# Four-layer GNN on one core: the first layer's edge stage in another order on ACT and DVE, and half of the prelude's one-hots of the high index part on POOL

## What is computed

```python
h = relu(layernorm(x))
x = x + L0(h, src, dst)      # degree-normalised convolution, l2 norm, tanh
h = relu(layernorm(x))
x = x + L1(h, ...)           # two relational attention layers
h = relu(layernorm(x)); x = x + L2(h, ...)
h = relu(layernorm(x)); x = x + L3(h, ...)

# L0
src_, dst_ = src + self loops, dst + self loops
deg  = segment_sum(ones, src_)          # a count of edges by source node
norm = rsqrt(deg)
agg  = segment_sum((h @ W)[src_] * norm[src_], dst_) * norm[:, None]
out  = tanh(agg / max(l2(agg), 1e-12))
```

## Time and profile before

| what | value |
|---|---|
| median of 3 runs | 4407.27 us (4401.42 to 4411.29) |
| the profiled execution | 4407.76 us, span 4406.1 us |
| mean granted TensorE clock | 0.829 |
| busy in the span | PE 68%, PEld 38%, DVE 78%, ACT 49%, POOL 47% |
| `prelude`, about 45 to 245 us | histogram loop 51 to 222 us |
| `layer0_edges`, about 597 to 1380 us | first scan 606.9 us, last `pq` 1372.0 us |

### The profile page before, as it was taken

One profiled execution on the slowest core, in us unless ns is written; L12 is line 12 of the kernel. 1 busy time (PEld: TensorE's weight loads), 2 busy tenths in 40 slices (PEclk: granted clock), 3 DMA queues, 4 the chain that ended last, 5 costly groups with the idle time before them and its releaser, 6 DMA issues. The chain is left out here.

```text
span 4406.1 us, 66823 instructions
## 1 busy us (share of the span) xinstructions
PE 2981.6 (68%) x12342; PEld 1689.0 (38%) x12342; DVE 3436.7 (78%) x10172; ACT 2152.9 (49%) x5600; POOL 2066.3 (47%) x1915
## 2 busy tenths in 40 slices
PE   5966644333344999567999322888887999707886
PEld 1255533222232444223444111544444666503443
DVE  6989968888886888675555686799995666698997
ACT  0058866666663222153212265677774666404554
POOL 0045567777774654005554000555555555204776
PEclk9967767777666999778999655899998999858999
DMA  2079966666663222174322297344444656503332
GB/s 51 2 223 309 310 212 225 212 210 213 212 225 101 68 63 59 24 213 118 64 62 57 79 246 203 101 131 123 128 126 149 201 192 198 163 0 114 114 113 87
DMA packets 621057, 628.07 MB, mean 143 GB/s; under 512 B 167332, under 2 KB 494590, under 8 KB 614468
## 3 DMA queue, kind: packets, MB, share of 16 engines
q1 hardware_dynamic: 572900, 523.78, 39.6%
q0 software_dynamic: 48000, 102.76, 9.5%
HBM read 333.97 MB, written 296.91 MB: 143 GB/s over the span
## 5 line engine op out<-in xcount | busy, mean ns | idle before, releaser
L1417 PE MATMUL r_pM<-r_masked,wr 128*128 128x512 f32 x1600 | 750.3, 622 | 55.3 <-DVE r_masked L1368 55.2
L1368 DVE SCALAR_TENSOR_TENSOR r_masked<-r_typ,r_hT 128x512 f32<-128x512 f32 x800 | 493.5, 687 | 239.9 <-ACT r_hT L1395 189.0
L1417 PEld LDWEIGHTS r_pM<-r_masked,wr 128*128 128x128 f32 x1600 | 308.8, 199 | 427.3 <-issue 298.5
L1259 PE MATMUL e_pY<-ident,e_agg 128*128 128x128 f32 x400 | 134.1, 439 | 406.8 <-DVE e_agg L1134 381.6
L741 POOL DMA_INDIRECT q_rows<-nr,row_x x200 | 258.0, 1290 | 194.8 <-PE q_pT L590 134.6
L2445 POOL DMA_INDIRECT out<-o_base,o_at_o x200 | 266.7, 1333 | 133.8 <-issue 66.3
L1259 PEld LDWEIGHTS e_pY<-ident,e_agg 128*128 128x128 f32 x400 | 107.0, 327 | 418.6 <-issue 234.5
L741 POOL DMA_INDIRECT r_xs<-tab,r_at_s x200 | 216.4, 1082 | 87.9 <-issue 46.3
L741 POOL DMA_INDIRECT r_xs<-h_tab,r_at_s x200 | 215.7, 1079 | 87.8 <-issue 47.0
L590 PE MATMUL g_pT<-ident,g_hT 128*128 128x128 f32 x400 | 95.2, 381 | 230.0 <-ACT g_hT L1799 177.1
L741 POOL DMA_INDIRECT i_hs<-hr,i_at_s x200 | 191.1, 956 | 88.0 <-issue 47.5
(11 more groups left out here) (416 smaller groups left out, 8943.0 us busy)
## 6 DMA issues: line engine op xcount, KB each, us to landing
xz<-na_xz SPq DMA_DIRECT2D x49, 1040.0 KB, 5.8
r_typ<-vec_s SPq DMA_DIRECT2D x100, 256.0 KB, 3.4
g_al<-alpha_s SPq DMA_DIRECT2D x100, 256.0 KB, 4.1
na_xz<-in_x SPq DMA_DIRECT2D x49, 512.0 KB, 7.0
tab<-na_x SPq DMA_DIRECT2D x49, 512.0 KB
e_xin<-tab SPq DMA_DIRECT2D x49, 512.0 KB
hr<-e_hh SPq DMA_DIRECT2D x49, 512.0 KB, 3.7
zh_s<-e_zh SPq DMA_DIRECT2D x49, 512.0 KB
```

What stands on the lines that cost most here:

```text
L1259: pe.matmul(pY[s][:, cols], agg[s][:, cols], g.ident[:, :], start=True, stop=False)
L1368: v.scalar_tensor_tensor(masked[:, r, :], typ[d.slot(4)][:, :], float(r), hT[d.slot(2)][:, :], ALU.is_equal, ALU.mult).then_inc(ev.mk, 1)
L1417: pe.matmul(pM[s][:, :], g.wr[:, layer * R_ + r, :], masked[:, r, :], start=(r == 0), stop=(r == R_ - 1)).then_inc(ev.mm, 1)
```

## The change

In `prelude` the loops on DVE and PE are written out for all 200 tiles. DVE no longer makes `hi1` of side 1. POOL makes it, one instruction per tile, once DVE has signalled the parts (`s_parts`) and, from tile 8 on, PE has done with the slot. PE waits for POOL's `s_hi` before side 1's product.

In `layer0_edges` the order of a turn changes on two engines. On DVE the pair's `n` moves behind `x1`, `sx` and `mx`. On ACT the chain `et` moves ahead, right behind `hh`; then come `hTx`, `rz`, `rh`, `by_dst`, the squares, and `pq` last. The waits of each step move with it.

```diff
@@ prelude
+        @block.gpsimd
+        def _(pool):
+            wait_alone(g, pool, s_parts, 1)
+            for t in range(T):
+                if t >= PER:
+                    wait_alone(g, pool, s_mm, 2 * (t - PER) + 2)
+                pool.tensor_scalar(hi1[:, t % PER, 1, :], g.iota_lo[:, 0:P], part[:, 0, 1, t:t + 1], None, ALU.is_equal).then_inc(s_hi, 1)
...
-            v.sem_inc(s_cmp, 2 * PER)
-            with v.Fori(0, T // PER) as i:
-                for k in range(PER):
-                    for side in range(2):
-                        v.wait_ge(s_mm, i * 2 * PER + 2 * k + side + 1)
-                        v.tensor_scalar(hi1[:, k, side, :], ...)
-                        v.tensor_scalar(lo1[:, k, side, :], ...).then_inc(s_cmp, 1)
+            v.sem_inc(s_parts, 1)
+            for t in range(T):
+                k = t % PER
+                for side in range(2):
+                    if t >= PER:
+                        v.wait_ge(s_mm, 2 * (t - PER) + side + 1)
+                    if side == 0:
+                        v.tensor_scalar(hi1[:, k, side, :], ...)
+                    v.tensor_scalar(lo1[:, k, side, :], ...).then_inc(s_cmp, 1)
...
+            for t in range(T):
+                k = t % PER
+                for side in range(2):
+                    if side == 1:
+                        pe.wait_ge(s_hi, t + 1)
+                    pe.wait_ge(s_cmp, 2 * t + side + 1)
+                    pe.matmul(ph[:, side, :], hi1[:, k, side, :], lo1[:, k, side, :], start=False, stop=False).then_inc(s_mm, 1)
@@ layer0_edges, DVE
-                if n2:
-                    ... normalise(v, hh[s][:, of(m), :], mvh[:, of(m), :], rh[:, of(m)], n_[s][:, of(m), :], nd.nn)
                 if e2:
                     ... x1, stats(v, c, g, x1[s], sx, mx, ed.sx)
+                if n2:
+                    ... normalise(...), as above
                 if n1:
                     ... nm
@@ layer0_edges, ACT (order within a turn)
-  rx, ri, by_src, hh, hTx, pq, rh, et, by_dst + squares, rz
+  rx, ri, by_src, hh, et, hTx, rz, rh, by_dst + squares, pq
```

More of the change, by code:

```diff
@@ L396, in prelude @@
         g.sem("nn_" + n) for n in ("zh", "cmp", "mm", "all", "vec", "deg", "norm", "sum", "pre", "row", "out", "turned"))
+    s_parts, s_hi = g.sem("nn_parts"), g.sem("nn_hi")
     PER = 8
@@ L494, in _ @@
             c.step(v.tensor_copy(part[:, :, :, :], part_i[:, :, :, :]))
-            v.sem_inc(s_cmp, 2 * PER)
-            with v.Fori(0, T // PER) as i:
-                for k in range(PER):
-                    for side in range(2):
-                        v.wait_ge(s_mm, i * 2 * PER + 2 * k + side + 1)
-                        v.tensor_scalar(hi1[:, k, side, :], g.iota_lo[:, 0:P], part[:, 0, side, bass.ds(i * PER + k, 1)], None, ALU.is_equal)
-                        v.tensor_scalar(lo1[:, k, side, :], g.iota_lo[:, :], part[:, 1, side, bass.ds(i * PER + k, 1)], None,
-                                        ALU.is_equal).then_inc(s_cmp, 1)
+            v.sem_inc(s_parts, 1)
[5 more added lines that the diff above has]
+                    if side == 0:
+                        v.tensor_scalar(hi1[:, k, side, :], g.iota_lo[:, 0:P], part[:, 0, side, t:t + 1], None, ALU.is_equal)
+                    v.tensor_scalar(lo1[:, k, side, :], g.iota_lo[:, :], part[:, 1, side, t:t + 1], None, ALU.is_equal).then_inc(s_cmp, 1)
             v.wait_ge(s_all, 2)
@@ L1171, in turn @@
                     stats(v, c, g, x1[s], sx, mx, ed.sx)
+                if n2:
+                    s = n2.slot(2)
+                    v.wait_ge(nd.rh, n2.one())
+                    if n2.k >= 2:
+                        v.wait_ge(w_n[s], 16 * n2.uses(2))
+                    for m in MEMBERS:
+                        normalise(v, hh[s][:, of(m), :], mvh[:, of(m), :], rh[:, of(m)], n_[s][:, of(m), :], nd.nn)
                 if n1:
@@ L1209, in turn @@
                         last.then_inc(nd.hh, 1)
[L1210 to L1222, removed]
                 if e2:
@@ L1230, in turn @@
                     a.activation(et[:, :, :], et[:, :, :], ACT.Exp, scale=-1.0, bias=g.log2_col[:, :]).then_inc(ed.r2, 1)
+                if e3:
+                    a.wait_ge(ed.tx, e3.now())
+                    a.wait_ge(ed.pq, e3.back(1))
+                    a.activation(hTx[:, :], pX[:, :], ACT.Relu).then_inc(ed.hx, 1)
+                if n1:
+                    a.wait_ge(nd.sz, n1.one())
+                    a.wait_ge(nd.hh, n1.back(1))
+                    rstd(a, g, c, mvz, rz, nd.rz)
+                if n2:
+                    a.wait_ge(nd.sh, n2.one())
+                    a.wait_ge(nd.nn, n2.back(1))
+                    rstd(a, g, c, mvh, rh, nd.rh)
                 if e1:
@@ L1239, in turn @@
                     last.then_inc(ed.ss, 1)
[L1240 to L1243, removed]
+                if e3:
+                    a.wait_ge(ed.pq, e3.now())
+                    if e3.k >= 2:
+                        a.wait_ge(w_q[e3.slot(2)], 16 * e3.uses(2))
+                    a.activation(pq[e3.slot(2)][:, :], pX[0:R_, :], ACT.Copy).then_inc(ed.pe, 1)
             braid.sweep(a, turn, c)
```

## The result

| | before | after | ratio, 95% interval |
|---|---|---|---|
| median | 4404.35 us (4 runs) | 4332.84 us (4 runs, 4325.94 to 4334.71) | 0.9833, 0.9815 to 0.985 |
| profiled execution, its span | 4407.76, 4406.1 us | 4331.46, 4329.7 us | |
| histogram loop, first low one-hot to last product | 51.2 to 221.6 us | 50.6 to 209.9 us | |
| woven stage, first scan to last `pq` | 765.1 us | 698.3 us | |
| last `pq` to the end | 3034.0 us | 3036.3 us | |

The span is 76.4 us shorter: 66.8 us in the woven stage, 11 us in the histogram loop, and nothing elsewhere beyond 2.3 us.

A forecast was written before the change was run, and what follows sets the result against it. DVE was taken as the bound in the histogram loop and woven stage, with 0.92 us a turn lost to ACT's order. 4407.8 - 69 (woven stage: -47 - 7 - 15) + 18 (prelude) = 4357 us, range 4305 to 4410.

The forecast's parts named there:

- DVE waits, -47: Woven stage: DVE's waits of `n` for `rh` and `x1` for `et` go in ordinary turns, minus 47 us, from 0.
- The end, -7: Last turns of the woven stage: with `et` first, DVE waits less for `rh` and `et`, minus 7 us, from 0 to 10.
- a new wait of about 0.8: Woven stage, turn before the last: the 3.3 us wait shrinks to about 0.8, giving 2.5 us.
- The loop, -15: DVE's loop branch in the woven stage: `n`'s eight instructions ahead of it cover part of the 3.9 us stall, minus 15 us.
- head start of 1.7 us: Woven stage: DVE's sequencer meets the branch before DVE is done, worth 1.7 us a pass, at most 2.2.
- Prelude, +18: Histogram loop: DVE loses one one-hot but pays 0.25 us for POOL's, 0.94 us a tile, plus 18 us over 200 tiles.
- rival B: Prelude costs more than the woven stage gives: at 1.3 us a tile 90 us longer, 4429 us; chance 0.12.
- ratio 0.84: Prelude: share of POOL's instruction that DVE can't overlap, 1.07/1.27, applied to an assumed 0.30 us.
- every case of two memory-reading instructions shown has them exclude each other: Prelude: reason for taking plus 18 us, between bounds of -33 us without exclusion and +88 us.
- Rival A: Prelude: DVE's and POOL's streams don't exclude each other, -33 in place of +18, 4306 us; chance 0.15.
- Rival C: Woven stage: POOL is the new bound, no turn under 13.3 us, 4388 us; chance 0.13.
- Rival D: Woven stage: the loop's stall goes altogether as written-out prelude code shifts the body, 20 us more, 4337 us; chance 0.10.

The follow-up runs named there:

- experiment 2: Kernel before with only DVE's new order in the woven stage: 4491.28 us; with only ACT's new order: 4378.15 us.
- Experiment 6: Changed kernel, POOL making three of four high one-hots, ACT's `rz` and `rh` ahead of `hTx` in turns without a new block: 4415.04 us, ratio 0.9967, other chip.
- experiment 4: With both on POOL: changed kernel, POOL making both high one-hots of every tile, DVE only the low ones: 4492.77 us on another chip.

## Why the prediction was right, point by point

**4357 us was forecast, 4333 measured**, inside 4305 to 4410, the woven stage as reckoned and the prelude with the wrong sign. The prelude was missed by 29 us, more than the whole; the range held that by its width:

| term | forecast | measured |
|---|---|---|
| waits of `n` and `x1`, the ordinary turns and the end | -47 - 7 = -54 | 35.2 + 21.8 - 8.1 - 2.6 = -46.3 |
| wait behind the branch | -15 | 34.8 - 23.2 = -11.6 |
| not in the sum: `nm` -7.0, `ssw` +4.8, DVE busy -7.6 | 0 | -9.8 |
| small waits | 0 | +0.9 |
| woven stage | -69 | -66.8 |
| prelude | +18 | -11 (0.806 against 0.863 per tile) |

- *DVE waits, -47.* Right, in mechanism and size: an ordinary turn lost 1.0 us (forecast 0.92), and experiment 2 shows that each order takes its own part and that DVE's half is a loss of 84 us without ACT's.
- *The end, -7.* Half of it. With the ordinary turns nearly clean, what is left of both waits (8.1 and 2.6) lies at the stage's ends: from the last scan to the last `pq` it went from 30.5 to 26.8 us, 3.7. The step that failed is "a new wait of about 0.8" for `n`: it was 3.86, since ACT comes to `rh` only behind `hTx`, and that waited 4.97 us for PE. Experiment 6 adds that the whole term could not be had by order: the stage's end follows the last gather.
- *The loop, -15.* The mechanism was right: the stall of about 4 us starts when the branch goes out and DVE's queued work covers part of it. So was the head start of 1.7 us: DVE's queued work ended 0.14 us behind the branch's start before, and 1.84 us behind it now. The term that failed is the stall itself, which the sum left as it was: from the branch's start to the sequencer's next record it is 4.30 us in the mean of nine now and was 3.89, so that 11.6/9 = 1.3 us a pass is left of the 1.7. It is 4.30 us with ACT's order alone too; why it grew stays open.
- *Missed rows.* One wait of 7.6 us of `nm` for `rz` was in the waits of before and in no step of the sum; moving `rz` ahead took it. And `z` beside `zh` lost less.
- *Prelude, +18.* Wrong, by two errors that pull apart. POOL's instruction is 0.60 us, not 0.30, which by the forecast's own formula would have been 0.69 + 0.50 = 1.19 us a tile and a loss of 68 us, the point at which rival B begins to win. But the ratio 0.84 is also wrong for this pair: it was taken from float32 sums of 128x512 and moved to fp16 comparisons. Measured it is 0.11/0.60. The step that failed is "every case of two memory-reading instructions shown has them exclude each other": the rows showed two pairs, neither of this form. In one of the two turns of rows 6 `z` kept its 1.28 us and it was POOL's `zh` that took 3.35, so even there DVE did not always pay. What came in its place is a shared pace of 0.79 us a tile, with 0.11 us lost to DVE.
- *Rival A* (no exclusion, -33) was the nearer one for the prelude: a third of its gain came. *Rival B* is the case of experiment 4 with both on POOL: there the pace is 1.26 us and the loop 82 us longer than before, near B's 90, with POOL as the bound and not the round trip that B described. *Rival C*: in the turns without a stall POOL has no gap either, with 8 gathers at 0.95 + 0.30 and 2.78 + 0.15 for `zh`, 12.9 us; the 13.3 of the forecast held a stretched `zh`. So POOL and DVE end together at 12.9 to 13.0, and the next gain in this stage has to shorten both. *Rival D*, the shifted code, did not happen in the changed kernel and did in two of the experiments on the first chip, whose stages are 24 and 29 us shorter; its time, 4337, is close to the result by chance.

## What to carry to other kernels

When a change reorders two engines, run each half alone: here one half of a good change makes the stage 84 us longer. DVE's loop body of 326 records paid about 4 us of its sequencer's time in each pass or nothing, depending on where it lay, so a change in an earlier stage can appear to cost or bring 24 us in a later one; look at the time from the branch to the next record before crediting the change. A ratio of contention read from one pair of instructions does not carry to another form: time the new instruction alone and beside its neighbour first.

## What the runs showed of the hardware

- A taken branch of DVE at the end of a body of 326 records: 2.75 to 5.8 us, mostly 4.2, to its sequencer's next record at places 248 to 2 of 256, and 0.22 to 0.26 us at 45 to 60 and 202.
- POOL's comparison of 128x128 fp16 against a column takes 0.60 us alone, 0.65 beside two DVE one-hots of 128x512, 0.81 beside those and one of 128x128, and up to 2.15 beside a DVE that is catching up. In the third case DVE's of 128x512 goes from 336 to 386 ns in the mean and its 128x128 from 237 to 271.
- DVE's `x1`, a sum of 128x512 float32, takes 1.7 us in place of 0.66 if it begins while POOL's sum of the same size runs; `z`, of the same size, mostly keeps its 0.68 us in that place, and POOL's sum is the longer one; beside a gather it keeps its 0.66 us, and the gather takes 1.43 us in place of 0.95.
- PE's matmuls of 128x512 fp16 in the histogram loop have a mean of 393 ns in the kernel after and 607 with both one-hots on POOL, at a granted clock of 1.00 in both. They are not PE's price: with operands ready they begin 0.22 us apart in the kernel after. The records are long where the next product comes late (0.63 us in place of 0.43); whether that is all of it was not tried.
